# Closing the last block of an optional pair ahead of the branch, and filling an idle TensorE in the first batch

## What is computed

```
Q, K  = ctx @ Wq.T, ctx @ Wk.T
sim   = Q K^T, scaled, 512 x 512 for each batch
thr   = 153rd largest value of each row of sim
A     = sigmoid(sim) where sim >= thr, else 0
x1    = x + (1 - g) * layernorm(x) + g * (A + A^T) / 2        g = sigmoid(gamma)
xn    = layernorm(x1)
top 2 of 8 experts for each row, by xn @ router_w.T
out   = x1 + sum over the 2 experts of weight * (silu(xn @ gate) * (xn @ up)) @ down
           + the same with one shared expert (704 wide, with biases)
```

## Time and profile before

| | |
|---|---|
| median of 3 runs | 537.44 us |
| the profiled execution | 537.37 us |
| its span, first to last instruction | 535.5 us |
| mean granted TensorE clock | 0.927 |
| TensorE busy (share of the span) | 456.4 us (85%) |
| VectorE busy | 351.6 us (66%) |
| ScalarE busy | 233.4 us (44%) |
| GpSimd busy | 189.8 us (35%) |

### The profile page before, as it was taken

The page is one execution under the profiler, slowest core; times in us unless marked ns, Lnnn a source line. Parts: engine busy times, 40 slices in busy tenths (PEclk is TensorE's granted clock), DMA queues, the critical chain, the costliest instruction groups (busy, mean ns, idle before and its releaser), DMA issues.

```text
span 535.5 us, 9441 instructions
## 1 busy us (share of the span) xinstructions
PE 456.4 (85%) x2794; PEld 256.5 (48%) x2795; DVE 351.6 (66%) x972; ACT 233.4 (44%) x410; POOL 189.8 (35%) x234
## 2 busy tenths in 40 slices
PE   6202687999999999999967999999999999999970
PEld 2100343445445544554434666666666666666630
DVE  4898999999999999936965555555556522332310
ACT  5563367247933793154514543444444322222210
POOL 2100230017001610080973355455445544544431
PEclk9655679999999999899988999999999999999976
DMA  8700450025402530247338777877877445444431
GB/s 278 224 1 1 163 172 1 2 78 166 92 1 78 118 42 1 80 106 122 101 111 221 207 179 176 180 191 178 207 180 196 81 78 84 88 83 94 85 63 20
DMA packets 39006, 60.55 MB, mean 113 GB/s; under 512 B 8233, under 2 KB 18729, under 8 KB 38962
## 3 DMA queue, kind: packets, MB, share of 16 engines
q0 software_dynamic: 10384, 23.38, 24.3%
q1 hardware_dynamic: 26514, 36.61, 21.4%
q10 hardware_dynamic: 2064, 0.02, 0.2%
HBM read 37.68 MB, written 22.30 MB: 112 GB/s over the span
## 4 chain that ended last, share of the span: by engine, by line
PE 51%; DVE 37%; issue 5%; ACT 2%; DMA 2%; POOL 1%; SPq 1%; DVEq 0%; POOLq 0%; ACTq 0%
DVE stats L1166 5%; PE bank L1086 4%; PE bank L1088 4%; PE bank L1087 4%; PE bank L1062 4%; PE bank L1066 4%; PE bank L1063 4%; PE bank L1067 4%; PE bank L1065 4%; PE bank L1064 4%; PE bank L1048 3%; DVE below L1207 3%; DVE sgt L1387 2%; PE bank L1075 2%; DVE top L1283 2%
## 5 line engine op out<-in xcount | busy, mean ns | idle before, releaser
L555 POOL DMA_INDIRECT out_dram<-xb,sidx x35 | 56.2, 1605 | 87.2 <-ACT xb L815 77.0
L928 PE MATMUL bank<-xT,W 128*128 128x512 f16 x176 | 67.5, 384 | 3.0 <-DVE sgt L1387 3.0
L1507 DVE TENSOR_TENSOR hS<-bank,hS 128x384 f16<-128x384 f32 x35 | 19.5, 558 | 74.8 <-ACT hS L807 74.8
L929 PE MATMUL bank<-xT,W 128*128 128x512 f16 x176 | 67.3, 382 | 0.0
L930 PE MATMUL bank<-xT,W 128*128 128x512 f16 x176 | 67.2, 382 | 0.0
L801 ACT ACTIVATE sgt<-bank 128x352 f32<-128x352 f32 x35 | 16.2, 463 | 88.7 <-PE bank L1067 88.7
L815 ACT ACTIVATE xb<-bank,wcol 128x512 f32<-128x512 f32 x35 | 24.0, 687 | 56.9 <-PE bank L1088 56.9
L490 POOL TENSOR_TENSOR rstd<-pw 128x4 f32<-128x4 f32 x12 | 16.1, 1345 | 87.8 <-DVE pw L1175 87.7
L1062 PE MATMUL bank<-W,xT 128*128 x140 | 44.1, 315 | 1.2 <-issue 1.1
L1063 PE MATMUL bank<-W,xT 128*128 x140 | 44.1, 315 | 0.0
L1067 PE MATMUL bank<-W,xT 128*128 x140 | 44.1, 315 | 0.0
(11 more groups left out here) (243 smaller groups left out, 1068.3 us busy)
## 6 DMA issues: line engine op xcount, KB each, us to landing
xn_dram<-W SPq DMA_DIRECT2D x16, 256.0 KB, 3.1
out_dram<-W POOLq DMA_DIRECT2D x12, 256.0 KB, 5.7
stage<-L_ffn_down_w_in SPq DMA_DIRECT2D x12, 256.0 KB
sim<-L_ffn_down_w_in SPq DMA_DIRECT2D x12, 256.0 KB
stage<-L_ffn_gate_w_in SPq DMA_DIRECT2D x16, 176.0 KB
stage<-L_ffn_up_w_in SPq DMA_DIRECT2D x16, 176.0 KB
sim<-L_ffn_gate_w_in SPq DMA_DIRECT2D x16, 176.0 KB
sim<-L_ffn_up_w_in SPq DMA_DIRECT2D x16, 176.0 KB
```

The lines of the kernel that those rows point to most:

```text
L928: pe.matmul(o, wh, xT[:, 0, c, :], start=(c == 0), stop=False)
L929: pe.matmul(o, wh, xT[:, 1, c, :], start=False, stop=False)
```

## The change

Two things are done.

In the optional pairs, the second block of a pair is closed inside the `If`, ahead of the next comparison and branch: a new function `close(j)` holds what `finish(j)` did on TensorE, VectorE and ScalarE, and the scatter on GpSimd. `rest` is told whether the last block was closed. If so, the first `step` behind the next branch (`alone`) leaves out what belongs to the block before, and the `Else` has nothing of it to do. GpSimd's `finish` still waits for the last transfers.

In batch 0, TensorE gets ten products of 128 x 128 by 128 x 512, whose result in bank 7 nobody reads: five after the scores of batch 1, one after each of the first two `transpose_xn`, three after the fourth. Ahead of them stands a wait for the first eight weight units (`s_wloD`, `EARLY`).

```diff
@@ gpsimd
-        def step(j, m, p, fetch=True):
+        def step(j, m, p, fetch=True, alone=False):
             if fetch:
                 pool.wait_ge(s_x2, j + 2)
                 gather(j + 3, 1 - p)
             if isinstance(j, int) and j == 0:
                 add_shared(NB - 1, TB - 1, ylasts[TB - 1])
-            else:
+            elif not alone:
                 scatter(j - 1, m if p else m - 1, 1 - p)
 
+        def close(j):
+            scatter(j, j // 2, j % 2)
+
         def finish(j):
-            scatter(j, j // 2, j % 2)
             for i in range(2):
                 pool.wait_ge(d_sc[i], 16 * ((j + 2 - i) // 2))
                 pool.wait_ge(d_xg[i], 16 * ((min(j + 3, BLOCKS - 1) + 2 - i) // 2))
@@ scalar
-        def finish(j):
+        def close(j):
             routed_h(j, j % 2)
             routed_y(j, j // 2, j % 2)
...
@@ tensor
+        def keep_busy(n):
+
+            for _ in range(n):
+                pe.matmul(bank[7][:, :], ident16[:, :], W[:, SG_HI:SG_HI + S], start=True, stop=True)
+
...
+            if b == 0:
+                pe.wait_ge(s_wloD, EARLY)
+                keep_busy(5)
             transpose_xn(b, 0)
+            if b == 0:
+                keep_busy(1)
             transpose_xn(b, 1)
             if b:
                 down_part(b - 1, 3, range(0, 3))
+            else:
+                keep_busy(1)
             transpose_xn(b, 2)
             transpose_xn(b, 3)
+            if b == 0:
+                keep_busy(3)
...
-            if not first_block:
+            if not first_block and not alone:
                 routed_hT(j - 1, 1 - p)
...
             if first_block:
                 shared_down(NB - 1, TB - 1)
-            else:
+            elif not alone:
                 routed_down(j - 1, 1 - p, where(j - 1))
...
-        def finish(j):
+        def close(j):
             routed_hT(j, j % 2)
             routed_down(j, j % 2, where(j))
...
@@ all engines
-def rest(eng, used, j, step, finish):
+def rest(eng, used, j, closed, step, close, finish):
 
     if j == BLOCKS:
         finish(j - 1)
         return
     with eng.If(used > j):
-        step(j, j // 2, j % 2, fetch=j + 3 < BLOCKS)
+        step(j, j // 2, j % 2, fetch=j + 3 < BLOCKS, alone=closed)
         step(j + 1, (j + 1) // 2, (j + 1) % 2, fetch=j + 4 < BLOCKS)
-        rest(eng, used, j + 2, step, finish)
+        close(j + 1)
+        rest(eng, used, j + 2, True, step, close, finish)
     with eng.Else():
+        if not closed:
+            close(j - 1)
         finish(j - 1)
```

More of the change, by code:

```diff
@@ L589, in finish @@
                 pool.wait_ge(d_xg[i], 16 * ((min(j + 3, BLOCKS - 1) + 2 - i) // 2))
-        run_blocks(pool, used, step, finish)
+        run_blocks(pool, used, step, close, finish)
     @block.scalar
@@ L826, in step, with finish @@
                 shared_out(NB - 1, TB - 1, ylasts[TB - 1])
-            else:
+            elif not alone:
                 routed_y(j - 1, m if p else m - 1, 1 - p)
         act.wait_ge(s_route, 1)
-        def finish(j):
+        def close(j):
             routed_h(j, j % 2)
             routed_y(j, j // 2, j % 2)
-        run_blocks(act, used, step, finish)
+        def finish(j):
+            pass
+        run_blocks(act, used, step, close, finish)
     @block.tensor
@@ L1109, in step, with finish @@
                 shared_down(NB - 1, TB - 1)
-            else:
+            elif not alone:
                 routed_down(j - 1, 1 - p, where(j - 1))
         routed_x(0, 0, 0)
-        def finish(j):
+        def close(j):
             routed_hT(j, j % 2)
             routed_down(j, j % 2, where(j))
-        run_blocks(pe, used, step, finish)
+        def finish(j):
+            pass
+        run_blocks(pe, used, step, close, finish)
     @block.vector
@@ L1530, in _, with close, run_blocks @@
         later_weights(sum(SECOND_AT) - 4)
+        def close(j):
+            routed_h(j, j % 2)
         def finish(j):
-            routed_h(j, j % 2)
-        run_blocks(dve, used, step, finish)
+            pass
+        run_blocks(dve, used, step, close, finish)
     es.close()
-def run_blocks(eng, used, step, finish):
+def run_blocks(eng, used, step, close, finish):
     for j in range(HEAD_BLOCKS):
@@ L1546, in run_blocks @@
         step(2 * i + (HEAD_BLOCKS + 1), i + (HEAD_BLOCKS // 2 + 1), 0)
-    rest(eng, eng.value_load(used, min_val=0, max_val=BLOCKS), SURE, step, finish)
-def rest(eng, used, j, step, finish):
+    count = eng.value_load(used, min_val=0, max_val=BLOCKS)
+    rest(eng, count, SURE, False, step, close, finish)
+def rest(eng, used, j, closed, step, close, finish):
     if j == BLOCKS:
```

## The result

| | before | after |
|---|---|---|
| median | 537.31 us (22 runs) | 535.77 us (22 runs) |
| ratio, 95% interval | | 0.9972 [0.9962, 0.9982] |
| the profiled execution | 537.37 us | 535.46 us |
| its span | 535.5 us | 533.6 us |
| mean granted clock | 0.927 | 0.933 |

The kernel is 1.5 us faster (1.0 to 2.0 by the interval). The forecast was 534.7 us in a range of 532.9 to 536.2: the sign is right and the time lies in the range, but only about half of the 2.7 us arrived.

The account below looks back on a forecast made before the run. It took the chain of waits to run through VectorE in the batches and TensorE in the blocks. 537.37 - 2.72 (end) + 0 (products) = 534.65, with the median 0.07 above: 534.7 us, range 532.9 to 536.2.

Parts of the forecast that it names:

- the 2.7 us: At the kernel's end, block 34's scatter was to start at 520.95 instead of 523.67: 2.72 us gained.
- The stall is the jump's, and it goes: Behind block 33: TensorE's 2.35 us idle at the branch vanishes; block 34's transposes start at 513.41 instead of 515.92.
- Rival E: At the branch: unloaded code, not the jump, stalls TensorE, so 2.35 us idle stays; 537.4 us, chance 0.04.
- The clock stays high in the closing: Block 34's down product to its scaling: 2.14 us at 2.4 GHz, 4.06 if the clock falls to 1.2.
- Next is the landing of block 33's scatter: At the end, block 34's scatter must wait until block 33's has landed, and so starts at about 520.95.
- Rival A: At the last scatter: no wait for block 33's scatter, clock high, 3.8 to 4.57 us gained; 532.9 to 533.7, chance 0.18.
- Its size: Between the last two scatters: last packet at 520.0 to 520.1, 0.45 us until GpSimd goes on, issue 0 to 0.86.
- Rival B: At the last scatters: the stalled branch's instruction fetch delays a landing by 1.1 us; 535.8 us, chance 0.11.
- Everything behind stays as it was: Behind the last scatter: landing and GpSimd's 6.73 us drain unchanged, its extra branch 37 to 50 ns, TensorE's stalls covered.
- The ten products cost 0, at most 0.3 us: In the batches: the products fit into TensorE's waits, cost 0, at most some 0.3 us, and gain 0.
- Rival C: Longer wait ahead of 87.71: clock falls, 2.0 us of products lost, 0.2 reaching the path; 534.9 to 536.7, chance 0.09.
- Rival D: Batch 1, 87.71 to 104: clock stays low, 8.2 us late, 6.4 on the path; 541.1 us, chance 0.03.

Follow-up runs that it names:

- experiment 4: Kernel before with the two sides of each If exchanged, so the closing lies in the side not jumped to: 534.95 us, ratio 0.9962.
- Experiment 3: Whole change plus eight more products between block 34's transposes and its down product, timed against the kernel before: 535.44 us, ratio 0.9973.
- experiment 1: Only the closing ahead of the branch, without the ten products, against the kernel before: 534.67 us, ratio 0.9953.
- experiment 2: Only the ten products in batch 0, added to the kernel before: 536.91 us, ratio 0.9988.
- experiment 6: Only the closing, with the last DMA waits moved from GpSimd to SyncE, against the kernel before: 532.32 us, ratio 0.9910.
- experiment 9: Only the closing, with TensorE waiting ahead of the branch for its own block's scatter to land, against the kernel before: 534.86 us, ratio 0.9946.

## Why the prediction was right, and where it was off

**The stall is the jump's, and it goes.** Right. Predicted: block 34's transposes 0.22 us behind the down product, L1105 2.2 behind the start of the last L1107 of block 33, no issue time ahead of L1094. Measured 0.21 and 2.22 (513.85 to 516.07). Rival E is refuted by the profile, and experiment 4 shows the mechanism without moving any code in front: only the jump over far code costs, 4.3 us, where a branch that reads on takes 0.07 and a jump over one closing 0.37. The Trainium skill, "Advanced Engine Details and Errata", Control Flow Timing, has about 108 ns for a compare and branch: this case is below it where TensorE reads on (70 to 75 ns) and on ScalarE and GpSimd throughout (34 to 54 ns), and 30 to 46 times above it for TensorE's far jump (3.3 to 4.95 us). The Trainium skill, "Runtime: NRT & Kernel Launch", Instruction fetch mechanics, says that a taken branch has to fetch its target first if that isn't in the loaded window. Experiment 4 agrees in that the near jump, at 0.37 us, stalls nothing and the far one takes 4.3 us; the size of a window no run here shows.

**The clock stays high in the closing.** It does: the down product takes 2.15 us from L1105 to the scaling (516.07 to 518.22, predicted 2.14).

**Next is the landing of block 33's scatter.** Right as a mechanism. Experiment 3 delays the closing by 1.6 us, and the last scatter still waits for the landing; experiment 1 without the products shows the same wait. Rival A (no such wait) didn't happen in any of eleven profiles.

**Its size is the term that was off.** I took 5.80 us from block 33's scatter to the last one (515.15 to 520.95), of which 5.35 were the landing until GpSimd sees it (520.05 + 0.45) and 0.45 the issue, a middle between 0 and 0.86. The chain after shows both apart: the landing takes 4.86 (515.82 to 520.68), and from there to the scatter's start it is 0.81 (to 521.49). So the issue was 0.4 us too short and the landing 0.5 too long, and in this one execution they nearly cancel, by luck: 5.67, and the end from block 33's scaling is 2.56 us shorter against 2.72 predicted. In eleven profiles the distance is 5.55 to 7.12, with a mean of 6.1, and the issue is 0.80 to 0.82 in each: the mean landing, 5.3, was right, and the issue is the term that was mis-sized. It was bounded from both sides, and the true value lay at the upper end. The rows had it: the 0.86 from the end of L815 to the scatter was nearly all issue, and stands ahead of block 33's scatter too (514.29 to 515.15). For kernels like the one after, with the jump beside the landing, the mean is 6.3 and the term 0.5 too small. Rival B gave 1.1 us to that collision; against the three kernels without it the scatters are 0.2 us further apart on average with one instruction packet beside the landing and 1.0 with two. Set against the 8.52 us before (515.15 to 523.67), a mean of 6.3 leaves 2.2 us of gain at the end, which is what experiment 1 measures (2.5, from 1.5 to 3.6).

**Everything behind stays as it was.** Right: the drain is 6727 ns; GpSimd's additional branch takes at most 53 ns. TensorE's jump ends at 520.3, far within the 533.4 at which the drain ends, as forecast.

**The ten products cost 0, at most 0.3 us.** Nearly. The first wait is filled as the sum had it, and the wait behind it grew to 4.72 us (forecast 4.3 or more). Rival C, which had a chance of 0.09, did happen: the clock fell in that wait and the products until 93.3 ran at 1.2 GHz. Its price on the path was forecast at 0.2 us if the reserves hold: VectorE's chain lost 0.05, 0.10 and 0.56 us in three profiles. That it is so near is luck. Behind the reserve of 1.24 us at L894 VectorE stood 0.6 to 1.1 us late, and 0.84 of that came back in four faster instructions that no sum had. The products alone gain 0.6 us by the ratio of experiment 2, within its interval of nothing; that they are worth anything isn't shown. Between the ratios of the whole change and of the closing alone lies 1.0 us, but the intervals overlap, and experiment 2's leaves a cost of at most 0.4.

Rival D's price was wrong by its own terms, though it didn't happen: 87.71 to 104 are 16.3 us of work at the high clock, so all of it at the low clock would come 16 us late and not 8.2. In the profile after, the low clock lasted for 4.9 us of products (88.39 to 93.3).

**So where did 1.2 us of 2.7 go?** 0.5 us into the distance of the two scatters (0.4 of it the issue), 0.2 into VectorE's chain (the mean of three). The rest, 0.5 us, is not settled: 2.7 less these two terms is 2.0 us, where the interval of the measured gain ends. Besides, executions of the same code differ in whether the clock falls at 291 to 295 us, which costs 1.7 us where it does; a profile shows one such execution, a median mixes them.

## What to carry to other kernels

A branch that jumps over much code can cost TensorE some microseconds and other engines nothing: read the sequencers' branches, and put what is on the critical path on the side that is read on, or in front. Before adding up such a gain, look for the next wait on the same result, and take its length from several instances of it; here a DMA landing and the issue behind it, 5.6 to 7.1 us where one row gave 5.8, took back about half of what the engines had gained. Products that keep the clock high in one wait can move the idle time into the next, and the clock can fall there: look at the next wait before filling one. And let an engine that has nothing else to do wait for the last DMA, if another has a long drain before it.

## What was not expected of the hardware

- GpSimd's drain at the end takes 6.73 us with no DMA packet in flight, in every kernel where GpSimd itself waits for the last landing, and the same time passes beside a landing DMA (8.67 us from the start of the last scatter's issue, in experiment 6). Moving the last wait to SyncE gave 2.3 to 2.5 us by the two comparisons, against 1.5 for the whole change.
- TensorE's far jump takes 3.5 us with nothing else on the DMA queues (experiment 9), and 3.3 to 4.9 us otherwise. The same branch takes 44 to 50 ns on ScalarE.
- The time from block 33's scatter to the last one, which waits for it, differs by 1.6 us over eleven kernels with one profile each. It goes with the number of instruction packets beside the landing (5.55 to 5.78 us with none, 6.41 to 7.12 with two), while the last scatter's own packets pass alike in all.
- The clock fell at the start of the blocks, between 291 and 295 us, in seven of nine profiles, and in the four with products that keep TensorE busy there it stayed at 2.4 GHz.
